# Graph convolutions on one core: TensorE multiplies a block of zeros with every tile

## The chip, the cores and the metric

The program runs on one core of a Trainium2 chip. Its time is in device microseconds (us), from one launch; less is better.

## The reference

Two graph networks follow each other over a graph of 6250 nodes with 128 features and 100,000 edges (`src`, `dst`, a type 0 to 7), each with a residual and a layer norm.

The first has three relational convolutions (between them a batch norm over the nodes and a ReLU):

```
weight = einsum('rb,bio->rio', comp_l, bases_l)      # 8 types from 4 bases
h      = einsum('ni,rio->nro', x, weight)
msg    = h[src, etype]
norm   = 1 / max(count of edges with this dst and type, 1)
agg    = segment_sum(msg * norm, dst)
out    = agg + x @ root_l + bias_l
```

The second projects to 64 features, then makes three hops. Row and column are here `src` and `dst`, and the weight is 1/sqrt(deg[row] deg[col]), deg the number of edges that leave a node:

```
h = x @ W_in + b_in
three times:  cur = segment_sum(cur[col] * edge_weight, row); acc += cur
out = acc / 4 @ W_out + b_out
```

## The kernel before

Nodes are columns: the features lie over the partitions, and the nodes (6250, padded to 6656) along the free dimension in 13 blocks of 512. A **setup** sorts the edges by the block of their target, for `dst` and later for `src`, into groups of 256 slots; two tiles of 128 edges make a group, 403 groups and 806 tiles in all. It also counts edges and finds each edge's weight. Slots are placed by indirect DMAs of GpSimd (line 454).

A **convolution** (there are six: k = 0 to 2 of the first network, 3 to 5 are the hops) goes through the 806 tiles in turns of 16 (the last has 6):

- GpSimd (`gather`, lines 462 to 473) fetches for each tile 128 rows of a table in DRAM, by an indirect DMA, into `msg[:, b]`. There are 16 such buffers. Gather n waits at line 470 until TensorE has signalled (`summed`) that the tile 16 before it is done, and at line 468, for each four tiles, for their row numbers, which ScalarE casts (line 505) once the four gathers of the turn before have landed.
- VectorE (`select`, line 1075) makes the tile's selection matrix `sel`: 128 edges x 512 nodes, one where the edge's target is that node (in the first three, times the edge's weight). There are 8 such buffers, and the one of tile n waits for `summed` of tile n - 8.
- TensorE (`turn`, lines 763 to 776) waits for the selection (766), for the gather (767) and, on even tiles, for a free accumulator (770), then multiplies messages by selection (line 771): 128x128 (64 columns in the hops) by 128x512 in f32, into one of four PSUM banks, 0 to 3. The two tiles of a group add up in one bank. Each product signals `summed`. In the trace such an f32 product is two weight loads and two matmuls.
- VectorE (`add`, line 1091) adds the finished bank to the sum of its node block. The order on VectorE is fixed: two selections of pair q, then the addition of pair q - 2. The addition waits for `summed` (line 1088).
- In the first three convolutions, the first 6 tiles of each turn carry another product (line 776, recorded at line 755): 125x49 by 125x128 in f16, which counts the edges that leave each node, into bank 7. VectorE makes its two operands (lines 1081 and 1082).

All instructions of a convolution are written out; each engine works its own in order. Between convolutions, TensorE makes the next message table (line 740) and the root product (line 751), or in the hops transposes; they use banks 0 to 6. Bank 6 is not touched while a convolution runs. `zeros16` is a 128x512 f16 block of zeros in SBUF, filled once by GpSimd; it also opens and closes the two long accumulations of counts.

Of the kernel before, what the change touches and what calls it, by code (L numbers as in the profile page):

```python
# [83 lines left out]
def build(nc, x, src, dst, etype, bases, comp, root, bias, bn_w, bn_b, w_in, b_in, w_out, b_out, out):  # L84
    with ExitStack() as ctx:
        def sb(name, shape, dt=F32):
            return ctx.enter_context(nc.sbuf_tensor(name, shape, dt))
# [53 lines left out]
        zeros16 = sb("zeros16", [128, BW], F16)  # L141
# [74 lines left out]
        psum = ctx.enter_context(nc.psum_tensor("psum", [128, 8, 512], F32))  # L216
# [52 lines left out]

        EMPTIES = ((edge_rows[E:2 * E, :], 2 * E), (placed["src"], 256 * NT), (placed["dst"], 2 * (128 * NT + E)))  # L270
        EMPTY_OUT = 16 * sum(len(fills(words)) for _, words in EMPTIES)
        PARAMS = 8 + LAYERS + 2 * (LAYERS - 1)
        blocks_of = [range(4 * m, min(4 * m + 4, NBLK)) for m in range(NXT)]


        def tiles(k, i, b=0):
            return NT * k + B * i + b

        def groups_of(k, i, q=0):
            return NG * k + Q * i + q  # L280
# [4 lines left out]
        def gathers(k, i, b):  # L285

            return 16 * ((NIT if b < LAST_B else NIT - 1) * k + i + 1)

        def turn_loop(engine, turn):

            for i in range(NIT - 1):
                turn(i, B)
            turn(NIT - 1, LAST_B)
# [347 lines left out]
        def _(pe):  # L641
            t = nc.tensor
# [101 lines left out]
            def root_product(layer, source):  # L744
# [3 lines left out]
                for c in range(NB):  # L748
                    if c >= 6:
                        pe.wait_ge(root_kept, NB * layer + c - 5)  # L750
                    t.matmul(psum[:, c % 6, :], root_sb[:, layer, :], source[:, chunk[c]], start=True, stop=True).then_inc(root_mm, 1)

            def degree(block, low, **flags):

                return t.matmul(psum[0:NBLK, 7, 0:128], block, low, skip_group_check=True, **flags)  # L755

            def conv(k):
                width = D if k < LAYERS else H
                if k < LAYERS:

                    pe.wait_ge(root_kept, NB * (k + 1))

                def turn(i, n):
                    for b in range(n):

                        pe.wait_ge(sel_ready, tiles(k, i, b) + 1)
                        pe.wait_ge(gathered[b], gathers(k, i, b))
                        if b % 2 == 0:

                            pe.wait_ge(added, groups_of(k, i, b // 2) + 1)  # L770
                        t.matmul(psum[0:width, b // 2 % PB, :], msg[:, b, 0:width], sel[:, b % SB, :],  # L771
                                 start=b % 2 == 0, stop=b % 2 == 1).then_inc(summed, 1)
                        if k < LAYERS and b < DC:
                            pe.wait_ge(degree_ready, DC * (NIT * k + i) + b + 1)
                            u = degree_hot[:, b, :]
                            degree(u[:, 0:NBLK], u[:, NBLK + 1:NBLK + 129], start=False, stop=False).then_inc(degrees, 1)
                turn_loop(pe, turn)
# [39 lines left out]

            pe.wait_ge(norms, WB + NCHUNK)
            degree(zeros16[0:EP, 0:NBLK], zeros16[0:EP, 0:128], start=True, stop=False)
            for layer in range(LAYERS):  # L820
                conv(layer)
                if layer < LAYERS - 1:
                    pe.wait_ge(weights_ready, layer + 2)
                    table_blocks(layer + 1, cur, 0, NBLK)
                    root_product(layer + 1, cur)
            degree(zeros16[0:EP, 0:NBLK], zeros16[0:EP, 0:128], start=False, stop=True).then_inc(degrees, 1)

            pe.wait_ge(added, PB + groups_of(LAYERS, 0))
# [435 lines left out]
```

## Time and profile before

| | us |
|---|---|
| Median of 3 runs | 8625.23 (8610.7 to 8629.0) |
| The profiled execution | 8602.98 |
| Its span, first to last instruction | 8601.2 |
| Around the span | 1.8 |
| Mean granted TensorE clock, of 2.4 GHz | 0.841 |
| TensorE busy (matmuls) / weight loads | 6088.5 / 2066.8 |
| GpSimd busy | 5966.9 |
| VectorE busy | 5032.0 |
| ScalarE busy | 793.9 |

PE is TensorE's matmuls, PEld its weight loads, DVE VectorE, ACT ScalarE, POOL GpSimd. A row of the timeline gives start, length, engine, line, operation, output and inputs, how many instructions in a row were merged, and in brackets how long the engine was idle before and what ended the wait. "issue" is that nothing in the profile ended it. "remote" is that the semaphore which ended the wait came over 1.5 us after the end of the last instruction that could have raised it, so the profile names none. Ends of matmuls are modelled; their starts are recorded.

### The profile page before, as it was taken

How to read it: one execution, taken by the hardware profiler on the slowest of the kernel's cores; microseconds unless marked ns; L12 is line 12 of the kernel's file. 1: busy time of each engine (PE TensorE's matmuls, PEld its weight loads, DVE VectorE, ACT ScalarE, POOL GpSimd, SP SyncE). 2: the span in 40 equal slices, each digit the busy share in tenths (PEclk: the TensorE clock that was granted, in tenths of full speed). 3: DMA queues.
4: the chain of work that ended last, by engine and by line, in shares of the span. 5: the costliest groups of instructions: out<-in, count | busy, mean ns of one | idle time of the engine just before them, and what ended most of it. 6: DMA issues, size and time to landing. Idle time of an engine off the chain costs nothing.

```text
span 8601.2 us, 79809 instructions
## 1 busy us (share of the span) xinstructions
PE 6088.5 (71%) x14111; PEld 2066.8 (24%) x14112; DVE 5032.0 (59%) x12874; ACT 793.9 (9%) x2392; POOL 5966.9 (69%) x5856
## 2 busy tenths in 40 slices
PE   7755047777778788777877867777677777677776
PEld 3233012222222222222222221111111111111111
DVE  8977036666646666636666665555555554555556
ACT  5822000000010000020000010000000000000000
POOL 3877776667777667776667647777677777677774
PEclk9955568888888888888888878889889888898998
DMA  5100011111241111241111211111211111211112
GB/s 192 25 4 1 1 26 46 47 46 46 51 130 46 47 46 46 43 141 46 47 46 47 46 32 24 23 23 23 29 23 24 24 23 23 36 23 23 23 24 30
DMA packets 239252, 354.33 MB, mean 41 GB/s; under 512 B 129737, under 2 KB 139802, under 8 KB 238414
## 3 DMA queue, kind: packets, MB, share of 16 engines
q0 software_dynamic: 180352, 239.74, 13.8%
q1 hardware_dynamic: 58396, 109.81, 3.8%
q8 instruction: 112, 1.84, 0.1%
q14 instruction: 262, 2.15, 0.1%
q10 hardware_dynamic: 130, 0.80, 0.0%
HBM read 258.83 MB, written 100.66 MB: 42 GB/s over the span
## 4 chain that ended last, share of the span: by engine, by line
PE 45%; issue 19%; POOL 18%; DVE 8%; another core or an unknown queue 7%; DMA 2%; DVEq 1%; POOLq 0%; ACT 0%; SPq 0%
PE psum L771 43%; POOL placed_src L454 11%; POOL msg L471 7%; DVE sel L1075 2%; DVE agg L1091 2%; DMA msg<-hop_table,stage_idx 2%; PE psum L755 1%; DVEq L1086 1%; DVE bufD L1081 0%; POOL stage_addr L449 0%; DVE bufE L931 0%; DVE node_stats L1152 0%; DVE bufD L1082 0%; DVE cur L1168 0%
## 5 line engine op out<-in xcount | busy, mean ns | idle before, releaser
L771 PE MATMUL psum<-sel,msg 128*128 128x512 f32 (+1 forms) x9672 | 5148.1, 669 | 2117.8 <-issue 1095.7
L1091 DVE TENSOR_TENSOR agg<-agg,psum 128x512 f32 (+1 forms) x2418 | 1642.1, 679 | 3306.5 <-PE psum L771 1607.5
L471 POOL DMA_INDIRECT msg<-hop_table,stage_idx x2418 | 2486.5, 1028 | 1094.6 <-issue 631.5
L471 POOL DMA_INDIRECT msg<-msg_table,stage_idx x2418 | 2414.2, 998 | 1050.3 <-issue 628.1
L771 PEld LDWEIGHTS psum<-sel,msg 128*128 128x128 f32 (+1 forms) x9672 | 1554.0, 177 | 4882.8 <-issue 3752.6
L1075 DVE TENSOR_SCALAR sel<-iota,slots,norm 128x512 f32<-128x512 f32 x2418 | 1304.1, 564 | 12.5 <-ACT agg L576 12.5
L454 POOL DMA_INDIRECT placed_src<-stage_pay,stage_addr x800 | 1022.0, 1278 | 304.9 <-issue 216.2
L1075 DVE TENSOR_SCALAR sel<-iota,slots 128x512 f32<-128x512 f32 x2418 | 1096.5, 492 | 0.1
L505 ACT CAST stage_idx<-slots 128x4 int32<-128x4 f32 x1212 | 232.9, 194 | 6979.9 <-DMA msg<-msg_table,stage_idx 3526.3
L755 PEld LDWEIGHTS psum<-bufD 125*49 125x49 f16 x918 | 95.5, 104 | 842.8 <-issue 683.0
L1122 DVE SCALAR_TENSOR_TENSOR cur<-iota,bufE,psum 128x128 f32<-128x128 f32 x808 | 234.6, 345 | 88.4 <-PE psum L703 56.9
L667 PE MATMUL psum<-bufE 125*128 125x392 f16 x800 | 208.2, 341 | 50.0 <-DVE bufE L1003 25.0
L1082 DVE TENSOR_SCALAR bufD<-iota,bufD 125x128 f16<-125x128 f16 x918 | 234.0, 255 | 0.0
L703 PE MATMUL psum<-bufE 96*128 x808 | 122.5, 307 | 157.3 <-ACT bufE L555 69.7
L1081 DVE TENSOR_SCALAR bufD<-iota,bufD 125x49 f16<-125x49 f16 x918 | 231.0, 252 | 0.0
L755 PE MATMUL psum<-bufD 125*49 125x128 f16 x918 | 229.5, 250 | 0.0
L1001 DVE TENSOR_SCALAR bufE<-iota,bufD 125x392 f16<-125x392 f16 x800 | 228.6, 335 | 0.7 <-PE psum L667 0.3
L740 PE MATMUL psum<-weights,cur 128*128 128x512 f32 x392 | 174.1, 606 | 25.0 <-ACT cur L601 23.7
L691 PE MATMUL psum<-ident,bufE 128*96 128x128 bf16 x808 | 131.6, 319 | 39.6 <-DVE bufE L1113 19.5
L533 ACT ACTIVATE bufE<-iota,bufD 125x128 f16<-125x128 f16 x500 | 155.4, 386 | 4.1 <-DVEq L993 4.1
L555 ACT CAST bufE<-psum 96x512 bf16<-96x512 f32 x202 | 117.2, 581 | 331.9 <-PE psum L691 274.9
L1055 DVE COPY sel<-psum 128x512 f32<-128x512 f32 x98 | 67.7, 691 | 111.2 <-PE psum L740 106.1
(176 smaller groups left out, 1613.0 us busy)
## 6 DMA issues: line engine op xcount, KB each, us to landing
msg_table<-sel SPq DMA_DIRECT2D x147, 512.0 KB
msg<-msg_table,stage_idx POOLq DMA_INDIRECT x2418
msg<-hop_table,stage_idx POOLq DMA_INDIRECT x2418
placed_src<-stage_pay,stage_addr POOLq DMA_INDIRECT x800
placed_dst<-edge_rows SPq DMA_DIRECT2D x13, 781.2 KB
hop_table<-sel SPq DMA_DIRECT2D x21, 224.0 KB, 2.8
bufE<-inv_sqrt SPq DMA_DIRECT2D x2, 1568.0 KB, 10.1
out<-cur SPq DMA_DIRECT2D x12, 256.0 KB
```

The costliest lines, as they stand in the source:

```text
L454: g.indirect_dma_start(out=placed[k][0:128 * NT, :], out_offset=bass.IndirectOffsetOnAxis(ap=stage_addr[:, c:c + 1], axis=0), in_=stage_pa ...
L471: g.indirect_dma_start(out=msg[:, b, 0:width], out_offset=None, in_=table, in_offset=bass.IndirectOffsetOnAxis(ap=stage_idx[:, b:b + 1], a ...
L505: a.copy(stage_idx[:, c * CH:(c + 1) * CH], slots[:, bass.ds(B * i + c * CH, CH), 0]).then_inc(staged, 1)
L667: return t.matmul(psum[:, 4, 0:R * NBLK], low, high, skip_group_check=True, **flags)
L755: return t.matmul(psum[0:NBLK, 7, 0:128], block, low, skip_group_check=True, **flags)
L771: t.matmul(psum[0:width, b // 2 % PB, :], msg[:, b, 0:width], sel[:, b % SB, :], start=b % 2 == 0, stop=b % 2 == 1).then_inc(summed, 1)
L1001: last = v.tensor_scalar(hot[:, u, 0:o], iota16[0:EP, 0:o], type_block[:, bass.ds(CU * i + u, 1)], None, ALU.is_equal)
L1075: v.tensor_scalar(sel[:, b % SB, :], iota[:, :], slots[:, column, 1], *weight).then_inc(sel_ready, 1)
L1081: v.tensor_scalar(u[:, 0:NBLK], iota16[0:EP, 0:NBLK], src_block[:, bass.ds(at, 1)], None, ALU.is_equal)
L1082: v.tensor_scalar(u[:, NBLK + 1:NBLK + 129], iota16[0:EP, 0:128], src_low[:, bass.ds(at, 1)], None, ALU.is_equal).then_inc(degree_ready, 1)
L1091: v.tensor_tensor(at, at, psum[0:width, q % PB, :], ALU.add).then_inc(added, 1)
L1122: last = v.scalar_tensor_tensor(out=unread[:, c * CH + j, :], in0=iota[:, 0:128], scalar=low_f[:, at], in1=psum[:, c, j * 128:(j + 1) * 12 ...
```

## The change

With every tile of the six convolutions, right behind its product, TensorE multiplies a 128x128 block of `zeros16` by all 512 columns of `zeros16`, in f16, and writes the result to PSUM bank 6, which nobody reads. The product waits for no semaphore and raises none. That is 806 x 6 = 4836 weight loads and as many matmuls.

```diff
@@ in the block of TensorE, ahead of degree() @@
+            def keep_warm(bank, times):
+
+                for _ in range(times):
+                    t.matmul(psum[:, bank, :], zeros16[:, 0:128], zeros16[:, :], start=True, stop=True)
+
@@ in conv(), turn() @@
                         t.matmul(psum[0:width, b // 2 % PB, :], msg[:, b, 0:width], sel[:, b % SB, :],
                                  start=b % 2 == 0, stop=b % 2 == 1).then_inc(summed, 1)
+                        keep_warm(6, 1)
                         if k < LAYERS and b < DC:
                             pe.wait_ge(degree_ready, DC * (NIT * k + i) + b + 1)
```

## Rows read from the trace of the kernel before

**Rows 1.** The page: busy time, the clock's 40 slices, the chain by engine.

```profile
PE 6088.5 (71%) x14111; PEld 2066.8 (24%) x14112; DVE 5032.0 (59%) x12874; ACT 793.9 (9%) x2392; POOL 5966.9 (69%) x5856
...
PEclk9955568888888888888888878889889888898998
...
PE 45%; issue 19%; POOL 18%; DVE 8%; another core or an unknown queue 7%; DMA 2%; DVEq 1%; POOLq 0%; ACT 0%; SPq 0%
```

**Rows 2.** Windows, one a convolution: length, busy by engine, clock, DMA share, GB/s.

```profile
1174.00:2337.00 1163.00, 918.44 (x1918) 334.41 (x1918) 734.95 (x1803) 39.62 (x199) 811.76 (x812) 0.86 0.19 46
...
5026.00:6182.00 1156.00, 833.20 (x1612) 215.14 (x1612) 599.28 (x1208) 38.32 (x198) 824.85 (x802) 0.87 0.12 23
...
7382.00:8539.00 1157.00, 825.50 (x1612) 214.53 (x1612) 601.12 (x1207) 38.34 (x198) 817.88 (x800) 0.89 0.13 23
sum 6957.00, PE 5257.16 PEld 1649.08 DVE 4007.93 ACT 231.25 POOL 4894.04; mean PE 876.19 PEld 274.85 DVE 667.99 ACT 38.54 POOL 815.67
```

**Rows 3.** Groups by line and shape: count, busy us, mean ns, idle before.

```profile
L771 PE MATMUL psum<-sel,msg 128*128 128x512 f32 x4836 | 2660.2, 682 | 1101.1 <-DMA msg<-msg_table,stage_idx 385.2 <-DVE sel L1075 383.0 <-issue 332.0
L771 PE MATMUL psum<-sel,msg 128*64 128x512 f32 x4836 | 2487.9, 656 | 1016.7 <-issue 763.7 <-DVE sel L1075 183.8 <-DMA msg<-hop_table,stage_idx 61.2
L471 POOL DMA_INDIRECT msg<-hop_table,stage_idx x2418 | 2486.5, 1028 | 1094.6 <-issue 631.5 <-PE psum L771 265.6 <-DMA hop_table<-sel 120.6
```

**Rows 4.** Waits: us in total, times, longest.

```profile
DVE agg L1091 <- PE psum L771: 1607.5, 740, 303.3
DVE agg L1091 <- remote: 1352.2, 249, 9.7
...
POOL msg L471 <- PE psum L771: 510.5, 586, 5.0
```

**Rows 5.** Timeline of a hop, 6428 to 6446 us.

```profile
6429.42 0.87 DVE L1075 TENSOR_SCALAR sel<-iota,slots 128x512 f32<-128x512 f32 x2
...
6429.95 3.67 PE L771 MATMUL psum<-sel,msg 128*64 128x512 f32 x4 [5.65 <-issue]
...
6434.76 0.95 POOL L471 DMA_INDIRECT msg<-hop_table,stage_idx  x1 [0.30 <-issue]
6436.01 0.94 POOL L471 DMA_INDIRECT msg<-hop_table,stage_idx  x1 [0.30 <-issue]
...
6437.26 0.94 POOL L471 DMA_INDIRECT msg<-hop_table,stage_idx  x1 [0.30 <-issue]
6439.31 0.68 DVE L1091 TENSOR_TENSOR agg<-agg,psum 64x512 f32 x1 [9.03 <-remote]
6439.44 1.07 POOL L471 DMA_INDIRECT msg<-hop_table,stage_idx  x1 [1.24 <-remote]
6439.92 0.87 DVE L1075 TENSOR_SCALAR sel<-iota,slots 128x512 f32<-128x512 f32 x2
...
6440.45 3.67 PE L771 MATMUL psum<-sel,msg 128*64 128x512 f32 x4 [6.83 <-issue]
```

**Rows 6.** Timeline of TensorE's matmuls in a dense stretch of the second convolution.

```profile
3105.07 9.71 PE L771 MATMUL psum<-sel,msg 128*128 128x512 f32 x22
3114.71 0.24 PE L755 MATMUL psum<-bufD 125*49 125x128 f16 x1
3114.88 1.13 PE L771 MATMUL psum<-sel,msg 128*128 128x512 f32 x2
3115.93 0.24 PE L755 MATMUL psum<-bufD 125*49 125x128 f16 x1
```

**Rows 7.** Timeline of TensorE's matmuls in the setup, clock at 1.00.

```profile
254.11 1.00 PE L667 MATMUL psum<-bufE 125*128 125x392 f16 x5 [0.21 <-issue]
...
268.72 0.34 PE L667 MATMUL psum<-bufE 125*128 125x392 f16 x1 [0.27 <-DVE bufE L1003]
```

**Rows 8.** Windows of four stretches of the second convolution, columns as in rows 2.

```profile
2991.00:3007.00 16.00, 14.38 (x35) 5.32 (x33) 9.88 (x28) 0.58 (x3) 12.04 (x14) 1.00 0.21 50
3008.00:3017.00 9.00, 4.99 (x6) 2.19 (x7) 5.91 (x12) 0.39 (x2) 5.02 (x5) 0.50 0.16 38
3018.00:3034.00 16.00, 14.76 (x36) 5.39 (x34) 9.77 (x27) 0.58 (x3) 12.34 (x13) 1.00 0.20 52
3035.00:3041.00 6.00, 3.86 (x5) 1.80 (x6) 4.79 (x9) 0.19 (x1) 2.84 (x4) 0.50 0.12 33
```

**Rows 9.** Timeline of the same place, 3000 to 3013 us.

```profile
2999.72 0.59 PE L771 MATMUL psum<-sel,msg 128*128 128x512 f32 x1
...
3010.63 0.69 DVE L1091 TENSOR_TENSOR agg<-agg,psum 128x512 f32 x1 [8.30 <-remote]
```

## The prediction

> **What bounds the kernel now.** I began with the page: busy shares and clock [rows 1]. No engine is full. Each digit of the clock line averages two levels, 1.2 and 2.4 GHz. The rows by convolution [rows 2] come next: the six take 6957 of 8601 us, a convolution of the first kind 1163 us, one of the second 1156. Over 806 tiles that is 1.44 us a tile whatever the kind, though the first kind also makes 306 degree products. The groups by shape [rows 3] price a tile's work. GpSimd's gather lasts 1.03 us on average and its successor starts 0.30 later (the 0.30 stands in [rows 5]); undisturbed, gathers follow each other every 1.25 us. So GpSimd alone would need 806 x 1.25 = 1008 us, and with the mean gather 1.33 x 806 = 1072. The rest of the 1156 to 1163 us is GpSimd held back, since gather n may not start before TensorE has signalled tile n - 16.
>
> TensorE's own pace is in [rows 6]: 22 matmuls of L771, two a tile, last 9.71 us, so with the last one's 0.59 us [rows 9] taken off they start every (9.71 - 0.59) / 21 = 0.434 us: 0.87 us a tile at the high clock. It is fast enough for the gathers, and it loses its lead in a way that the waits show [rows 4]: VectorE stands 1352 us in 249 waits ahead of its additions (5.4 us each) until a signal comes whose matmul had by the record ended long before. [Rows 5] hold such a case. TensorE's matmuls from 6429.95 end at 6433.62 and nothing follows until 6440.45; yet the addition at 6439.31, and the gather at 6439.44, start only then. GpSimd meanwhile issued gathers 1.25 us apart. VectorE can't make the next selection behind that addition, TensorE starves, and its clock drops: 4 matmuls take 3.67 us there, and [rows 8] have 0.50 of the clock right behind two such idle times and 1.00 in the dense stretch between. Then TensorE catches up at 0.87 against the gathers' 1.25 to 1.4. **Its slack is what repairs each stall.**
>
> **The change, part by part.** Nothing is removed or moved. Each tile gets one more weight load and one more f16 product of 128x512: 6 x 806 = 4836. It waits for nothing. It is issued behind the tile's own signal, so it delays no signal of its own tile, but every later one; queued behind it are the next tile's two waits and the degree product. Bank 6 is read by nobody while a convolution runs. VectorE, ScalarE, GpSimd and every DMA keep their instructions.
>
> Price of one product. Low end: the f16 products of 392 columns start (1.00 - 0.34) / 4 = 0.165 us apart [rows 7], where 0.34 is the length of one alone [rows 7]; scaled to 512 columns 0.22. High end: in [rows 6] a tile with a degree product takes 1.22 us (3114.71 to 3115.93), 0.35 more than one without, though it streams only 128 columns. Leaving the f32 stream and coming back costs most of it. With 384 more columns at 0.165 / 392 each (0.16) the new product costs 0.51. The high end is taken: same type, same place in the stream. Below nothing has no ground: the work can't vanish from an in-order engine. A tile then takes 0.87 + 0.51 = 1.38 us, with a degree product behind it in the same type 1.43 (only its 128 columns, 0.05) or at worst 1.73 (its full 0.35).
>
> TensorE's need at the high clock: first kind (10 x 1.38 + 6 x 1.43) / 16 = 1.40 us, x 806 = 1127; at worst 1.51 x 806 = 1218; second kind 1112. At the low price 1.09 x 806 = 879. Against 1163 and 1156 TensorE goes from having two fifths of its time to spare to having 3%.
>
> The waits then. Today's 1352 us are 225 us, some 42 waits, a convolution. With 1.38 against GpSimd's 1.33 a stall is no longer repaired: its length stays in the total. Bounds: all of them stay (225 us each) or none. The late signals stand where GpSimd gathers unhindered, and a slower TensorE holds GpSimd back on most tiles, so I let a fifth stay: 45 us, 8 waits, and behind each about two tiles at the low clock, 2 x 1.38 = 2.8 us more, 22 us. A convolution of the first kind becomes 1127 + 67 = 1194 (+31), of the second 1179 (+23); 3 x 54 = **+162 us**. The clock gives nothing beyond this: the products come only with tiles, and leave the idle times as empty as before. Another way to the size: 306 degree products go with 7 us more a convolution [rows 2], 0.023 us each for 0.35 us of TensorE; 4836 x 0.023 = +111. I take +135.
>
> The profiled execution took 8603.0 us, 1.8 around its span; the median of the runs shown is 8625.2, 22 more. 8625 + 135 = **8760**.
>
> **Rivals.** *A. TensorE sets an even pace, and that is faster.* If holding GpSimd back removes all late signals, TensorE never starves, stays at 2.4 GHz and its 1127 and 1112 us are all: 3 x -36 + 3 x -44 = -240, 8385. It decides from the point where no addition waits for a late signal. For it: in dense stretches signals are prompt and the clock is 1.00 [rows 8]. Against: the late signals begin in dense stretches too (the addition at 3010.63 in [rows 9] waited 8.30 us and stands right behind the first of them), and nothing shows that the gathers cause them.
> The page "TensorE: Matmul & The Clock Gate" of the Trainium skill, under "Why this matters for your kernels", advises against idle gaps between bursts of matmuls; by it, dense work is the gain here, while the gaps of [rows 5] stay between tiles.
> *B. It is absorbed.* If the product costs near its low end, a tile takes 1.09 us, still under every gather pitch, and the stalls are repaired as now: 8625, or up to +111 by the degree products. The idle time before L771, 2118 us in [rows 3], speaks for room. This is also what comes out where the change doesn't do what it says: same gaps, same clock, same time.
> The same page, under "Back-to-back issue gap", gives N / 2.4 + 2.5 ns for matmuls in a row, an estimate of 216 ns for 512 columns. [Rows 7] agree (0.22); the degree rows speak for more where types alternate. By the page the sum is case B's.
> *C. The stalls stay and nothing repairs them.* With half the waits left: 112 + 21 x 2.8 = 171 us over the need, 1298 and 1283, so 3 x (135 + 127) = +786, 9410; with the waits made longer by more instructions waiting to be signalled, more. For it: the page's chain has TensorE on 45% of the span [rows 1]. Against: GpSimd is held back sooner.
>
> **How the numbers follow.** Forecast 0.42, A 0.21, B 0.17, C 0.20. The range reaches from A's 8385 to between the forecast and C: 8390 to 9200, leaving out some 0.06 below and 0.13 above. The likeliest case alone holds 8640 to 8900. A measurement of this kernel can tell about 0.2% (17 us) from no change. Faster: A and a little of B, 0.24; within: half of B and the forecast's edge, 0.13; slower: 0.63.
>
> **What the profile will show.** Step by step: one more group of 4836 f16 matmuls and a tile's pitch of 1.38 us in a dense row (A, C and forecast), or 1.09 (B); VectorE's waits for late signals down from 249 to some 50 (forecast), near none (A), over 100 (C); granted clock over the convolutions above the 0.86 to 0.89 of now (forecast about 0.95, A 1.00, B unchanged, C lower); GpSimd's waits for L771 up from 511 us. The forecast is wrong if a dense tile takes under 1.2 us, or if the waits for late signals don't shrink.

## The result and the profile after

The changed kernel takes 8706.85 us (8696.4 to 8715.8, 4 runs) where the kernel before, measured beside it, takes 8622.33: ratio 1.0099, 95% interval 1.0082 to 1.0117, **84.5 us slower**. The profiled execution took 8709.53 us with a span of 8707.8, 106.6 more than the span of before. The mean granted clock rose from 0.841 to 0.913. One execution in this study, of the kernel with half the message product below, took 15470 us at a mean granted clock of 0.223 and is left out of the comparisons; the other nine of that kernel lie within 8667 to 8684.

The page of the changed kernel: the same three parts as in [rows 1].

```profile
PE 7234.2 (83%) x18947; PEld 2314.4 (27%) x18948; DVE 5016.2 (58%) x12874; ACT 794.3 (9%) x2392; POOL 5975.9 (69%) x5856
...
PEclk9955579999989999989999989999999999999998
...
PE 68%; POOL 12%; issue 7%; DVE 7%; another core or an unknown queue 5%; DVEq 1%; DMA 0%; POOLq 0%; ACT 0%; SPq 0%
```

TensorE has 4836 more matmuls and 1146 more busy us, and the clock line shows nines where it had eights. The other engines did what they did before. The chain that ended last runs through TensorE on 68% of the span, against 45%. By that share alone TensorE looks like the new bound; the experiments below show that it mostly is not.

Windows of one convolution each, against [rows 2] (length; busy by engine as TensorE, weight loads, VectorE, ScalarE, GpSimd; clock; DMA share; GB/s).

```profile
1188.00:2366.00 1178.00, 1038.27 (x2724) 396.79 (x2724) 737.06 (x1803) 39.63 (x199) 809.79 (x818) 0.96 0.18 45
5076.00:6253.00 1177.00, 1099.14 (x2418) 233.85 (x2418) 595.80 (x1208) 38.31 (x198) 826.93 (x802) 0.97 0.11 23
...
sum 7058.00, PE 6415.60 PEld 1897.11 DVE 3998.57 ACT 231.30 POOL 4894.12; mean PE 1069.27 PEld 316.19 DVE 666.43 ACT 38.55 POOL 815.69
```

The six convolutions take 101 us more than the 6957 of before: nearly the whole loss. It is even: 15 us in the one window and 21 in the other, where the first kind also has its degree products. The clock over the six is 0.95 to 0.98 instead of 0.86 to 0.89.

Timelines of two dense stretches of TensorE, one of the first kind and one of a hop, against [rows 6].

```profile
3005.16 1.02 PE L776 MATMUL psum<-sel,msg 128*128 128x512 f32 x2
3006.01 0.38 PE L756 MATMUL psum<-zeros 128*128 128x512 f16 x1
3006.23 1.02 PE L776 MATMUL psum<-sel,msg 128*128 128x512 f32 x2
3007.09 0.38 PE L756 MATMUL psum<-zeros 128*128 128x512 f16 x1
3007.30 1.02 PE L776 MATMUL psum<-sel,msg 128*128 128x512 f32 x2
...
6313.08 1.07 PE L776 MATMUL psum<-sel,msg 128*64 128x512 f32 x2
6314.09 0.39 PE L756 MATMUL psum<-zeros 128*128 128x512 f16 x1
6314.40 1.07 PE L776 MATMUL psum<-sel,msg 128*64 128x512 f32 x2
```

A tile of the first kind starts every 1.07 us, a tile of a hop every 1.32. Before, both took 0.86: in dense stretches the recorded starts of the matmuls lie 0.43 us apart, two a tile (the prediction's 0.87 comes from merged rows). So the same product costs 0.21 us in the one and 0.47 in the other. In the first kind the kernel's own matmuls load 128 columns of weights, as the zeros do; in the hops they load 64, and the zeros 128. In the hops nine tiles in ten start 1.32 us after the one before; the rest of a hop, some 110 us, is in few and longer gaps.

The waits, against [rows 4] (us in total, times, longest).

```profile
DVE agg L1097 <- PE psum L776: 2477.0, 1080, 329.1
POOL msg L471 <- PE psum L776: 625.5, 701, 3.5
DVE agg L1097 <- remote: 599.5, 150, 11.5
```

VectorE's waits for late signals ("remote", signals that come over 1.5 us after the end of what could have raised them) fell from 1352 us in 249 to 600 us in 150, while its waits for TensorE's products rose by 870. The sum of the two hardly moved: 2960 before, 3077 after. GpSimd waits for TensorE 625 us, not 511. The late signals themselves are still there, in the hop's timeline:

```profile
6336.29 0.68 DVE L1097 TENSOR_TENSOR agg<-agg,psum 64x512 f32 x1 [6.82 <-remote]
...
6337.42 1.07 PE L776 MATMUL psum<-sel,msg 128*64 128x512 f32 x2 [3.08 <-DVE sel L1081]
```

An addition stands 6.82 us, and TensorE then stands 3.08 us for the selection that VectorE makes behind it. The product of zeros can't fill that gap, since it comes with a tile.

### The profile page after: what moved, and what is told of

It reads as the page before. It is cut to its first block, busy times and chain, and to the rows that moved or that the text cites. A ratio compares the mean times of both kernels' runs of the same rounds, so it can differ in the third digit from the quotient of the medians.

```text
span 8707.8 us, 89481 instructions
## 1 busy us (share of the span) xinstructions
PE 7234.2 (83%) x18947; PEld 2314.4 (27%) x18948; DVE 5016.2 (58%) x12874; ACT 794.3 (9%) x2392; POOL 5975.9 (69%) x5856
## 3 DMA queue, kind: packets, MB, share of 16 engines
q0 software_dynamic: 180352, 239.74, 13.0%
## 4 chain that ended last, share of the span: by engine, by line
PE 68%; POOL 12%; issue 7%; DVE 7%; another core or an unknown queue 5%; DVEq 1%; DMA 0%; POOLq 0%; ACT 0%; SPq 0%
PE psum L776 53%; PE psum L756 13%; POOL placed_src L454 11%; DVE sel L1081 2%; DVE agg L1097 2%; PE psum L760 2%; DVEq L1092 1%; POOL msg L471 0%; POOL stage_addr L449 0%; DVE bufE L937 0%; DVE node_stats L1158 0%; DVE cur L1174 0%; DVE cur L1238 0%; POOL stage_pay L450 0%
## 5 line engine op out<-in xcount | busy, mean ns | idle before, releaser
L776 PE MATMUL psum<-sel,msg 128*128 128x512 f32 (+1 forms) x9672 | 5359.7, 637 | 1081.3 <-DVE sel L1081 508.2
L776 PEld LDWEIGHTS psum<-sel,msg 128*128 128x128 f32 (+1 forms) x9672 | 1329.4, 167 | 2356.1 <-issue 1542.7
L756 PE MATMUL psum<-zeros 128*128 128x512 f16 x4836 | 1896.9, 392 | 0.0
L756 PEld LDWEIGHTS psum<-zeros 128*128 128x128 f16 x4836 | 474.5, 98 | 2634.7 <-issue 2634.7
L1081 DVE TENSOR_SCALAR sel<-iota,slots 128x512 f32<-128x512 f32 x2418 | 1075.4, 483 | 0.1
```

Source lines behind the costliest of these rows:

```text
L756: t.matmul(psum[:, bank, :], zeros16[:, 0:128], zeros16[:, :], start=True, stop=True)
L1081: v.tensor_scalar(sel[:, b % SB, :], iota[:, :], slots[:, column, 1], *weight).then_inc(sel_ready, 1)
```

## The experiments

The main question: does the loss come from TensorE's longer tile, which takes the slack that repaired stalls (the prediction's theory, "theory 1" below), or from the number of instructions, whatever their length? Beside it: what sets the price of a product, the f16 type or the number of weight columns? Each expectation tells its theories anew. Each batch ran on one chip, with the kernel before timed beside it; the trace of it that is shown belongs to the first pair of runs, so convolutions are compared within a batch where that is possible. "A convolution" below is the time from its first to its last matmul of messages: 1162 (first kind) and 1156 us (hops) before, 1177 and 1175 after.

### First batch: length, count and place (before: 8695.7 us)

**A product a quarter as long.**

```diff
-t.matmul(psum[:, bank, :], zeros16[:, 0:128], zeros16[:, :], start=True, stop=True)
+t.matmul(psum[:, bank, 0:128], zeros16[:, 0:128], zeros16[:, 0:128], start=True, stop=True)
```

> The zero product has 128 columns instead of 512; its count, 4836, and its place stay. Theory 1 (TensorE's lost slack: what counts is how much of the 1.43 to 1.44 us a tile TensorE is busy): 384 columns less are 0.16 us less a tile, a dense tile of a hop goes from the changed kernel's 1.33 to 1.17 us, and most of the +85 us goes: +0 to +30 against the kernel before. Theory 2 (each TensorE instruction more makes late signals later, whatever its length): the number of instructions is the same, so the whole +85 us stays.

Measured: 8769.74, ratio 1.0090 (1.0073 to 1.0107), +74 us. A dense tile took 0.97 us in the first kind and 1.16 in the hops, 0.10 and 0.16 less than in the changed kernel; the loss stayed. The row of the waits:

```profile
DVE agg L1097 <- remote: 1013.5, 233, 10.3
```

It is VectorE's wait for late signals. They are nearly all back, 1014 us in 233 waits, and yet the time is the same. Theory 1 had +0 to +30 and missed. The length of the product doesn't set the loss, unless the shorter tile and the returned late waits happen to cancel; the kernels of the second batch speak against that.

**Two products a tile.**

```diff
-                        keep_warm(6, 1)
+                        keep_warm(6, 2)
```

> Two zero products of 512 columns with every tile. Theory 1: the second one follows in the same type and costs its columns alone, 0.22 us; a dense tile of a hop takes 1.54 us, over the 1.43 of now, so TensorE sets an even pace, the clock is 1.00 through the convolutions, additions hardly wait for late signals, and the time is 6 x 806 x 1.54 to 1.62 in the convolutions in place of 6957: +500 to +850 us. Theory 2: the second costs as the first did, +170 us in all, and late signals grow.

Measured: 9007.88, ratio 1.0365 (1.0348 to 1.0382), some 312 us over before. Windows of a convolution of the first kind and of a hop:

```profile
1187.00:2391.00 1204.00, 1165.57 (x3528) 467.57 (x3529) 741.82 (x1802) 39.97 (x199) 814.16 (x819) 1.00 0.18 45
5150.00:6402.00 1252.00, 1245.62 (x3223) 245.50 (x3224) 614.33 (x1208) 38.65 (x198) 798.72 (x802) 1.00 0.11 22
```

And the timeline of TensorE in a dense stretch of a hop:

```profile
5500.91 0.60 PE L756 MATMUL psum<-zeros 128*128 128x512 f16 x2
5501.45 1.07 PE L776 MATMUL psum<-sel,msg 128*64 128x512 f32 x2
5502.45 0.60 PE L756 MATMUL psum<-zeros 128*128 128x512 f16 x2
```

In the hops TensorE is the bound: a hop's tile takes 1.54 us, 806 x 1.54 = 1241 of the 1252 us, the clock is 1.00, and only 24 late waits are left. This is case A's even pace, and it is slower. Neither expectation met the time: theory 1 had +500 to +850, since it took a hop's 1.54 us for both kinds where the first kind needs 1.29 (1.66 with a degree product), and theory 2 had +170. The second product in a row costs 0.22 us (1.54 - 1.32), in hops too: what follows a product with the same weight columns is cheap.

**The product in the hops alone.**

```diff
-                        keep_warm(6, 1)
+                        if k >= LAYERS:
+                            keep_warm(6, 1)
```

> The zero product only in the three hops. In the changed kernel the three first convolutions take 13 to 15 us more each and the three hops 16 to 21. Both theories: +50 to +58 us, the hops as in the changed kernel and the first three as before. A rival, that what one convolution does to the clock or the signals carries over into the next, would give another split.

Measured: 8746.5, ratio 1.0051 (1.0032 to 1.0070), half the loss for half the products. The three convolutions without the product took 1173 to 1177 us, where those of the run with the short product took 1185 to 1194. This run's hops took 1182 to 1187, where the next run's, without any, take 1161 to 1164. So the loss is made convolution by convolution and in both kinds.

**Half the work for TensorE.** The kernel before, its message product on 256 of the 512 columns; half of each block's sums is left out.

```diff
-t.matmul(psum[0:width, b // 2 % PB, :], msg[:, b, 0:width], sel[:, b % SB, :],
+t.matmul(psum[0:width, b // 2 % PB, 0:256], msg[:, b, 0:width], sel[:, b % SB, 0:256],
```

> The kernel before, with every message product on half of its 512 columns (the other half of each block's sums is left out), so TensorE needs 0.43 us a tile in place of 0.87. If TensorE's length has any part in the pace of 1.43 to 1.44 us a tile (its cold starts, its catching up), the convolutions shrink, towards GpSimd's 1.25 to 1.33 us a tile: -480 to -900 us. If the pace is set elsewhere, and TensorE's slack before was large enough to cost nothing, as theory 1 has it, they stay at 1.43 to 1.44: within 40 us of the kernel before.

Measured: 8676.28, ratio 0.9981 (0.9971 to 0.9991).

```profile
2508.00:3682.00 1174.00, 706.08 (x1918) 383.06 (x1918) 729.65 (x1802) 38.34 (x198) 814.59 (x811) 0.68 0.18 46
6259.00:7422.00 1163.00, 664.55 (x1612) 236.92 (x1612) 593.97 (x1208) 38.32 (x198) 829.29 (x802) 0.63 0.11 23
```

TensorE is busy 706 of 1174 us, against 918 of 1163 [rows 2] (the lower clock takes back half of the saving), and that clock is 0.68 and 0.63, nearer 1.2 than 2.4 GHz; the kernel gains 19 us. So **TensorE's pace and its clock are not what the kernel before waits for**: 468 us of slack instead of 245 give next to nothing, and a clock lower by a fifth to a quarter costs nothing. It doesn't speak against theory 1, whose expectation was this very result (within 40 us, since the slack before was ample already).

### Second batch: what an instruction costs (before: 8619.7 us)

If not the length, then the number of instructions, TensorE's alone or anybody's. Three kernels of this batch change the number and try to change little else; the fourth changes the bytes of the gathers.

**Two short products a tile**, 19344 more instructions with their weight loads, of 32 columns each.

```diff
-t.matmul(psum[:, bank, :], zeros16[:, 0:128], zeros16[:, :], start=True, stop=True)
+t.matmul(psum[:, bank, 0:32], zeros16[:, 0:128], zeros16[:, 0:32], start=True, stop=True)
...
-                        keep_warm(6, 1)
+                        keep_warm(6, 2)
```

> Two zero products of 32 columns with every tile: 19344 TensorE instructions more, but hardly any array time (a dense tile of the first kind about 1.08 us, of a hop 1.25, both far under 1.43). Theories 3 and 4 (count): +150 to +170 us. Theory 1 (length): +0 to +20.

Measured: 8740.69, ratio 1.0138 (1.0121 to 1.0155), +121 us. Each product has a sixteenth of the columns, there are twice the instructions, and the loss is larger than the change's. Theory 1 had +0 to +20 and missed by far; theories 3 and 4, which go by the count, had +150 to +170 and missed too, by less. A dense tile takes 1.00 us in the first kind and 1.15 in the hops, as with the one product of 128 columns (0.97 and 1.16), which lost 74. Late waits are much alike as well, though on another chip:

```profile
DVE agg L1097 <- remote: 1009.3, 217, 13.0
```

So at nearly the same length of a tile, and the same late waits, twice the instructions cost 47 us more.

**No message product.** The kernel before with one f16 product of zeros in place of each message product: 9672 instructions fewer (an f32 product is two matmuls and two weight loads), and the messages are not multiplied.

```diff
-t.matmul(psum[0:width, b // 2 % PB, :], msg[:, b, 0:width], sel[:, b % SB, :],
+t.matmul(psum[0:width, b // 2 % PB, :], zeros16[:, 0:width], zeros16[:, :],
```

> The kernel before, with the f32 message product replaced by one f16 product of zeros (messages and selections are made and waited for, but not multiplied): one weight load and one matmul a tile in place of two and two. Theories 3 and 4: 9672 TensorE instructions less are -75 to -85 us. Theory 1, TensorE's length: no effect, as with half the width. If the time does not move, it is not the count of instructions either.

Measured: 8565.32, ratio 0.9934 (0.9918 to 0.9951), -54 us, at a mean clock of 0.537; theories 3 and 4 had -75 to -85, theory 1 nothing. The time lies between them. A window over the gathers of the first convolution:

```profile
1187.00:2333.00 1146.00, 518.27 (x1094) 117.87 (x1094) 717.35 (x1787) 39.23 (x197) 813.74 (x804) 0.50 0.18 46
```

TensorE is busy less than half of the time, all of it at 1.2 GHz, and the gathers still take 1149 us from the first to the last (1155 before). **GpSimd's gathers and what they wait for pace the convolutions**; TensorE adds little to them. Late waits of VectorE fell to 81 (368 us) here, and the time hardly followed; but 2017 us of its waits have no releaser in this profile (336 before), so more of them may hide there.

**The instructions on an idle engine.** Two 1-column copies a tile on ScalarE, which is busy 9% of the time: 9696 instructions written out, and a wait for every eight.

```diff
+                act.wait_ge(tiny, made[0])
+                made[0] += 1
+                for j in range(2 * CH):
+                    last = a.copy(scratch[:, j:j + 1], eps[:, 0:1])
+                last.then_inc(tiny, 1)
```

> The kernel before, with two one-column copies on ScalarE for every tile (9696 instructions, behind the casts of line 505, on an engine that is idle 90% of the time). In the runs so far 4836 weight loads and 4836 matmuls cost 75 to 85 us, about 8 ns an instruction, whether the matmuls had 128 or 512 columns. Theory 3 (the pace of 1.44 us a tile belongs to something that all engines' instructions load): +75 to +85 us here too. Theory 4 (only TensorE's instructions count, in its own signalling): within 17 us of the kernel before.

Measured: 8662.83, ratio 1.0045 (1.0028 to 1.0061), +43 us, for copies whose results nobody reads and that take 187 ns each on ScalarE. Both expectations missed: +75 to +85 if all instructions count alike, within 17 if TensorE's alone do. TensorE and its stream are untouched, so no theory that goes by TensorE's time gives this loss.

The copies stand ahead of ScalarE's next casts, for which GpSimd waits: that would be another way to lose time. The trace gives it little room. GpSimd waited 60.6 us for casts instead of 5.8, but 48 of them are two starts of a hop, where it otherwise waits for its table (75.4 us instead of 120.6). What did grow is the late waits: 310 in 1663 us on VectorE, against 277 in 1497 in the next run, on the same chip and with none added in the convolutions. And ScalarE, which in this run waits for its own signal ahead of every eight copies, got it late too:

```profile
6172.66 0.19 ACT L513 COPY scratch<-eps 128x1 f32<-128x1 f32 x1 [1.20 <-issue]
...
6179.03 0.66 ACT L513 COPY scratch<-eps 128x1 f32<-128x1 f32 x6 [4.12 <-remote]
6179.14 0.68 DVE L1100 TENSOR_TENSOR agg<-agg,psum 64x512 f32 x1 [6.97 <-remote]
6179.27 1.07 POOL L473 DMA_INDIRECT msg<-hop_table,stage_idx  x1 [1.21 <-remote]
```

The copy at 6172.66 is the last of its eight and raises the signal; the next eight start 6.2 us after its end, within 0.3 us of VectorE and GpSimd. There are 83 such waits of ScalarE (224 us, the longest 6.5). **So it isn't TensorE's signals alone that come late**: in such a stretch ScalarE's own do too, and three engines are released together.

**Half a gather.** 64 rows a tile; the other 64 partitions stay zero and their messages are left out.

```diff
-g.indirect_dma_start(out=msg[:, b, 0:width], out_offset=None
+g.indirect_dma_start(out=msg[0:64, b, 0:width], out_offset=None
...
-IndirectOffsetOnAxis(ap=stage_idx[:, b:b + 1], axis=0)
+IndirectOffsetOnAxis(ap=stage_idx[0:64, b:b + 1], axis=0)
```

> The kernel before, with each gather fetching 64 rows in place of 128 (the other 64 partitions of the message buffers stay zero), so half of the packets and half of GpSimd's descriptors go; every engine's instruction count stays. Theory 3 and a variant of it, that the gathers' packets are most of the shared load: the convolutions fall well under 1.43 us a tile, and late signals vanish (waits of additions on remote signals from some 250 to under 50). Theory 4: late signals stay as they are; the time falls only as far as the gather itself gets shorter, and is then bound by the late signals.

Measured: 8631.73, ratio 1.0009 (0.9998 to 1.0021), no difference. Its waits:

```profile
DVE agg L1092 <- PE psum L772: 1568.5, 746, 316.4
DVE agg L1092 <- remote: 1497.0, 277, 9.7
```

The gather fell from 1.03 to 0.99 us and carried half the bytes, but its queue moved as many packets as before, 180352. The late signals stayed. Theory 4's expectation was met: bytes are not what the late signals come from. Packets were not tested by this.

### Third batch: on a chip without late signals (before: 7930.7 us)

This chip ran the unchanged kernel in 7930.7 us (7915.2 to 7940.8, 13 runs), 8% below the other chips, more than any edit of this study moves.

**Eight rows a gather**, the same edit as above with 8 for 64; 120 of each 128 messages are left out. It was meant to cut the packets.

> The kernel before, with each gather fetching 8 rows in place of 128 (the other 120 partitions of the message buffers stay zero). With 64 rows the traced packets stayed 180352, at half the bytes, and so did the time. With 8 rows some of the 16 DMA engines have no row to move, so the number of packets itself should fall, by my estimate from 48 to about 32 a gather. Theory 3 (a shared load in which every instruction and every DMA packet counts): late signals nearly vanish (additions waiting on remote signals, some 250 to 280 now, under 80), and the convolutions go from 1.43 to 1.44 us a tile to GpSimd's 1.25 to 1.33: -500 to -900 us. Theory 6 (extra instructions cost only because they are fetched, and the pace of the convolutions is something else): within 60 us of the kernel before.

Measured: 7640.42, ratio 0.9637 (0.9621 to 0.9653). The packets stayed at 180352 again, which is 32 for each of the 4836 + 800 indirect DMAs, not the 48 of the expectation. So its premise failed, both expectations missed (-500 to -900, or within 60; measured -290), and the question stays open. What it does show is the pace: convolutions took 982 to 1000 us, where they take 1016 to 1072 in the next run, and the mean gather 920 (first kind) and 935 ns (hops), there 952 and 1022. A gather with a sixteenth of its rows saves less than a tenth of its time.

**The same copies in a loop**: nearly the same two copies a tile on ScalarE, in a loop of eight, which adds 119805 - 79809 = 39996 executed instructions but fewer written ones.

```diff
+                act.wait_ge(tiny, 8 * made[0])
+                made[0] += 1
+                with act.Fori(0, 8) as j:
+                    a.copy(scratch[:, bass.ds(j, 1)], eps[:, 0:1]).then_inc(tiny, 1)
```

> The kernel before, with the same two one-column copies a tile on ScalarE as in the run that cost 43 us, but as a loop of 8 turns behind each cast: 9696 copies executed as there, plus the loop's own branches, from a seventh or less of the written-out instructions. Theory 3 (executed instructions count): at least +43 us, more with the branches. Theory 6 (fetched instructions count): under +20 us.

Measured: 7926.38, ratio 0.9994 (0.9984 to 1.0004). Free, but on a chip where the written-out form was not run, and the loop is not small either: queue q14, one of the two that carry instructions, moved 310 packets, 48 more than before, where the written-out copies made it 76 more. So the pair is **inconclusive** as to whether fetched or executed instructions count. It stands for the kernel before on this chip. Its waits:

```profile
DVE agg L1099 <- PE psum L779: 2563.5, 2359, 339.5
POOL msg L473 <- PE psum L779: 806.0, 2645, 0.3
```

And its windows, one of each kind:

```profile
2358.00:3377.00 1019.00, 916.76 (x1918) 275.24 (x1918) 740.88 (x1802) 336.67 (x1782) 772.11 (x810) 1.00 0.21 53
5706.00:6777.00 1071.00, 832.35 (x1612) 157.47 (x1610) 623.85 (x1207) 336.98 (x1783) 818.63 (x801) 1.00 0.13 25
```

There is no row for late signals at all. GpSimd waits 2645 times and never over 0.3 us, the clock is 1.00, and a tile takes 1.26 us in the first kind and 1.33 in the hops: the gathers' own mean of 0.95 and 1.02 us and the 0.30 between them. Most of what the 1156 to 1163 us of before have on top goes with the late signals; in the first kind some 35 of the 145 us are longer gathers (a mean of 1.00 us before, 0.95 here).

**The product with the tile's own number of weight columns**: the changed kernel, with 64 columns of zeros as weights in the hops.

```diff
-t.matmul(psum[:, bank, :], zeros16[:, 0:128], zeros16[:, :], start=True, stop=True)
+t.matmul(psum[0:columns, bank, :], zeros16[:, 0:columns], zeros16[:, :], start=True, stop=True)
...
-                        keep_warm(6, 1)
+                        keep_warm(6, 1, width)
```

> The changed kernel, with the zero product in the three hops on 64 columns of weights, as the message product has there, and on 128 in the first three as before. In the changed kernel a dense tile takes 1.07 us in the first kind, where both products have 128 columns (+0.216 us), but 1.33 in the hops, where they have 64 and 128 (+0.47 us). If the step between column counts is what costs the 0.25 us, a dense tile of a hop now takes 1.07 us. Theories 3 and 6: the number of instructions is the same, so the time is that of the changed kernel, +70 to +90 us. Theory 1 (TensorE's length): the hops' part of the loss, some 50 us, goes.

Measured: 7974.25, ratio 1.0053 (1.0037 to 1.0070), +44 us. The timeline of a dense stretch of a hop:

```profile
5999.59 1.02 PE L776 MATMUL psum<-sel,msg 128*64 128x512 f32 x2
6000.44 0.38 PE L756 MATMUL psum<-zeros 128*64 128x512 f16 x1
6000.66 1.02 PE L776 MATMUL psum<-sel,msg 128*64 128x512 f32 x2
```

And a window of each kind:

```profile
2370.00:3402.00 1032.00, 1012.05 (x2724) 374.00 (x2724) 741.87 (x1803) 38.33 (x198) 784.88 (x812) 1.00 0.21 52
5742.00:6816.00 1074.00, 978.11 (x2418) 252.85 (x2418) 622.74 (x1210) 38.34 (x198) 821.29 (x802) 1.00 0.13 25
```

Where hop tiles follow without idle time they now start every 1.07 us, as in the first kind, instead of 1.32. The zeros start 0.85 us behind the tile, not 1.01. **The extra 0.25 us is the change of the number of weight columns, 64 to 128 and back, and not the change from f32 to f16**, which this kernel makes as often. On this chip, against the run with copies in a loop, the first kind loses 12 to 13 us a convolution and the hops 1 to 4. TensorE is within 20 us of filling the first kind's window there (1012 of 1032, in which its degree tiles take 1.44 us, longer than a gather), and a hundred short of it in the hops (978 of 1074).

By its expectation this run speaks against the count: that had +70 to +90 whatever the columns, and theory 1 had about +35. Each hop has the same 1612 instructions more as a convolution of the first kind, and loses almost nothing. So on the chip without late signals added instructions cost the hops under 3 ns each, and the loss sits where TensorE's tiles are longer than a gather. That is theory 1's mechanism, but it is a reading of one run there.

### The change once more

The changed kernel, unedited, on another chip with late signals (before: 8681.31 us).

> The changed kernel once more. The last three runs were on a chip where the kernel before takes 7931 us instead of 8620 to 8696, and where no trace holds a late signal. On a chip with late signals (kernel before near 8650): +75 to +95 us, additions waiting on remote signals at some 150, as at first. On a chip without (kernel before near 7930): by the run with equal column counts the first kind goes from 1.26 to 1.28 us a tile, +13 us a convolution; in the hops a dense tile costs TensorE 1.33 us, the very pace of GpSimd there, so each gets 5 to 25 us longer: +55 to +115 us in all. Were the late signals the reason of the loss (theory 3), it would be under +20 us there.

Measured: 8765.18, ratio 1.0102 (1.0085 to 1.0119), +84 us; clock 0.913. Its waits for late signals:

```profile
DVE agg L1097 <- remote: 596.5, 132, 11.7
```

The loss, the clock and the 600 us of late waits are all repeated, as expected for such a chip.

### Where the loss goes with

| edit | instructions | us | ns each |
|---|---|---|---|
| the change | +9672 | +84.5 | 8.7 |
| product of 128 columns | +9672 | +74 | 7.7 |
| two products of 32 columns | +19344 | +121 | 6.3 |
| the product in the hops alone | +4836 | +51 | 10.5 |
| copies on ScalarE | +9696 | +43 | 4.4 |
| one f16 product for the message's | -9672 | -54 | 5.6 |
| copies in a loop, chip without late signals | +39996 | -4 | 0 |
| equal weight columns, same chip | +9672 | +44 | 4.5 |
| half the columns of the message product | 0 | -19 | |
| two products of 512 columns | +19344 | +312 | 16.1, TensorE-bound |

On the chips with late signals, and up to the point where TensorE's tile is longer than the pace of the gathers, the loss goes with the number of instructions written into the program, 4 to 11 ns for each, and hardly with the columns they stream. The two rows from the chip without late signals don't carry this: there the hops lost nearly nothing. What links count and loss is open. The page's transfers on the instruction queue rise with the count, 112 packets before, and here after the change:

```profile
q8 instruction: 150, 2.46, 0.1%
```

The columns are packets, MB and share. The 38 more packets (0.62 MB) go with the 9672 more instructions; the run with ScalarE's copies has its extra 0.62 MB on the other instruction queue, 338 packets instead of 262. That a fetch delays a signal is not shown, and the trace speaks against the simplest form of it: of the 211 late waits over 2 us of VectorE in the convolutions of the kernel before, 28 overlap a packet of the two instruction queues, where packets spread at random would meet some 60 (an estimate from their number and the length of the waits). The spread of more than a factor of two between the rows of the table is also unexplained.

## Why the prediction was right, and where its reasons were not

**The sign and the size** came out, +84.5 against +135, the size with luck, as shown below. Of the likeliest case, a fair part of the picture did too: TensorE's stretches longer, the clock over the convolutions at 0.95 to 0.98 (0.95 forecast), GpSimd's waits for TensorE up (511 to 625), late waits fewer. They went to 150, not to 50.

**What bounds the kernel now: right in the main.** The 1072 us that GpSimd needs by its mean gather in a hop were measured in the hops on the chip without late signals (1066 to 1072), and most of the rest goes with the late signals. That the 1008 us of undisturbed gathers meet the first kind there (1016 to 1019) is luck: they were read from a hop, and the first kind's gathers are shorter (0.95 us). TensorE's pace of 0.87 us a tile holds to 0.01, but "two fifths of its time to spare" forgets the first kind's degree tiles: with them it needed (10 x 0.86 + 6 x 1.22) / 16 x 806 = 802 of 1163 us, under a third to spare.

**The price of a product: right in the hops, wrong in the first kind.** The high end, 0.51, was taken for both. Measured are 0.47 in the hops and 0.21 in the first kind, the low end of 0.22. The step that failed is "leaving the f32 stream and coming back costs most of it": the degree tiles from which it was taken change both the type and the number of weight columns, 128 to 49. In the hops it is the second that costs; for the degree product, which also waits for VectorE, it wasn't tried alone, but 128 f16 columns behind 128 weight columns cost 0.11 us (the short product, first kind) and the degree product 0.36. The forecast's 1.43 us for a tile with both meets the measured 1.44 by luck: its parts were 0.51 and 0.05, measured 0.21 and 0.37.

The Trainium skill ("TensorE: Matmul & The Clock Gate", "Back-to-back issue gap") gives N / 2.4 + 2.5 ns, 216 ns for 512 columns, which that section calls the gap of an isolated matmul; the first kind and the second of two products in a row agree with it (0.21 and 0.22). It doesn't speak of the change of columns, so by it the hops would be 0.25 us a tile too cheap. The prediction's own mark for being wrong, a dense tile under 1.2 us, was met in half of the convolutions (1.07): by its own terms the forecast's mechanism was wrong there.

With the prices put right, TensorE needs (10 x 1.07 + 6 x 1.44) / 16 x 806 = 974 us in the first kind and 1.32 x 806 = 1064 in the hops, both with 100 us and more to spare (17% and 9%). So the forecast's "3%" never came about, and the 1127 + 67 = 1194 and 1179 of the sum came close to the measured 1177 and 1175 by two errors that cancel: too high a need, and too few waits left.

**"Its slack is what repairs each stall": not borne out.** The forecast and case C followed from the lost slack. The product of a quarter of the columns kept the loss with more slack (+74 for an expected +30 at most), two of 32 columns each lost 121 for an expected 20 at most, and copies on ScalarE cost 43 without touching TensorE. Half the message product, with nearly twice the slack and 19 us gained, fits either reading. What was called another way to the size, 0.023 us for each degree product and so +111, was the nearest to the result. It can be read as a count of instructions, though it was read as TensorE's time (VectorE's two operands of each degree product are in it too). It was set beside the sum and should have been asked what it measures.

**"The clock gives nothing beyond this": right, and more so than said.** The clock went from 0.841 to 0.913 and the kernel lost 1%; at 0.66 (half the columns) and 0.54 (no message product) nothing was lost. The Trainium skill's advice against idle gaps ("TensorE: Matmul & The Clock Gate", "Why this matters for your kernels") brought nothing here: no run shows a gain in time from the higher clock.

**Rival B** had "8625, or up to +111 by the degree products", and its low price was right in half of the convolutions; the result lies inside its numbers. Against it: the clock and the late waits did change. **Rival A** was tried by the two products a tile: late waits near none (24), clock 1.00, and the hops TensorE-bound at 1252 us. The even pace exists, but it came only with tiles of 1.43 us (the mean of the first kind, 10 of 1.29 and 6 of 1.66) and 1.54, as long as the 1.44 us of the gathers with their late signals or longer, which is a loss in itself. **Rival C** would have had over 100 late waits and 786 us; there were 150, and 84.5; the run with the short product had 233 and lost less, so the number of late waits is not what makes the total.

**What stays open.** Why signals come late, those of ScalarE with TensorE's, and not on every chip. Why each written instruction costs nanoseconds there, or whether something else that goes with the count does. How the unedited change does on a chip without late signals: only the form with equal columns was run there, +44 us. From the hops' 1.32 us a tile, just under the 1.33 of the gathers, a little more than that is likely, but it was not measured. No version faster than the kernel before came out of the product: the shorter one, the one in the hops alone and the one with equal columns lose too.

## What to carry to other kernels

Before adding work that is to keep TensorE's clock up, halve TensorE's real work and see whether the time follows: if the clock falls and the time stays, the clock is worth nothing there, and filler that is issued only with a tile leaves the gaps empty anyway. A matmul put into a stream cost about its columns when it loaded as many weight columns as its neighbours, and 0.15 to 0.25 us more where it loaded 128 and they 64. And count instructions as well as busy time: on the chips with late signals, 10,000 more beside this kernel's 80,000 went with half a per cent on an idle engine and one on TensorE.

## What was not expected of the hardware

- The same kernel takes 8620 to 8696 us in four sets of runs and 7930.7 in a fifth, on another chip. The convolutions hold all of it (about 3 x 146 + 3 x 86 = 696 us), and what differs most in their waits is signals that reach an engine several us after the recorded end of what raised them (1352 us in 249 waits of VectorE, the longest 9.7): in the three traces of the fifth set there are none. They are not TensorE's alone: ScalarE got its own late 83 times (224 us) in the run with copies. An edit is to be judged only against the kernel before on the same chip.
- A change between 64 and 128 weight columns, there and back, costs TensorE 0.25 us in a stream of matmuls around a product of 512 columns (0.19 around one of 128, 0.15 around two of 32); a change between f32 and f16 alone costs nothing that shows (0.21 us for 512 columns of f16 between f32 products).
- 9696 one-column copies on an engine that was busy 9% of the time cost the kernel 43 us on a chip with late signals.
- An indirect gather of 128, 64 and 8 rows takes 1.03, 0.99 and 0.94 us in the hops, and 32 packets each time.
